# The clamp before the reciprocal norms: from VectorE's queue to GpSimd's

## The chip, the cores and the metric

One NeuronCore of one Trainium2 chip runs the whole program. The metric is the device time of one execution, in microseconds (us). In the profile the engines are called PE (TensorE's matmuls), PEld (its weight loads), DVE (VectorE), ACT (ScalarE), POOL (GpSimd) and SP (the queue that issues DMAs). L607 means line 607 of the kernel before.

## What is computed

The reference is a stack of four layers over x of 2 x 1024 tokens with 128 channels, each followed by a residual and a layer norm: attention, a mixture of experts, a state-space scan with a depthwise convolution, and a second mixture of experts with a shared expert. The change lies in the attention, which has 16 heads of 64 channels:

```python
def _l2norm(t):
    n = jnp.linalg.norm(t, axis=-1, keepdims=True)
    return t / jnp.maximum(n, 1e-12)

q = _l2norm(q) * jnp.exp(scale)
k = _l2norm(k)
sim = jnp.einsum('bhid,bhjd->bhij', q, k)
attn = jax.nn.softmax(sim, axis=-1)
out = jnp.einsum('bhij,bhjd->bhid', attn, v)
return out.transpose(0, 2, 1, 3).reshape(b, s, -1) @ w_out + b_out
```

The kernel computes 1 / max(n, 1e-12) as max(n squared, 1e-24) to the power -0.5. The maximum is the clamp that this case is about.

## The kernel before, in words

The function `attention` gives each engine one program of its own (one queue, carried out strictly in order) and ties them together by counting semaphores; the function `mixtures` does the other three layers behind it, in the same way. `Constants` holds small loads and tables that are made on the way.

The attention runs over pairs of heads (i from 0 to 7), each pair in 32 slots, that is 16 slots a head. A slot is one piece of the softmax: 256 queries against 512 keys. In each slot PE makes the scores into the PSUM bank pair SC (`scores`, L408 and L409), ACT takes the exponential into Pr (`exps`, L547), DVE takes the low half of the probabilities into Pl (`low_probs`, L644, one instruction of 128x1024), and three slots later PE multiplies Pr and Pl with the values into OP (`av`, L434 and L436, LAG = 3). SC has two buffers, Pr and Pl have PB = 5, and OP has two. After every second slot DVE reads OP (`read_out`: the reciprocal of the denominators L663 and the sum of the two parts L665), and POOL divides (`divide`, L756). The outputs are turned (L444), copied by ACT (L536), multiplied with w_out (`out_product`, L451) and added into x by DVE (`add_out`, L671); the next `out_product` and the next projection use the same bank M0 and wait for that addition.

Between these, all engines prepare the next head. PE projects q, k and v in eight pieces (`proj`, L375 to L377), ACT copies them to raw (L516) and squares them (L517), and the rest goes in four groups g. For each group DVE sums the squares (`square_sums`, L603) and clamps the sums (L607), POOL takes the power (`inverse_norms`, L764), DVE normalises (`normalize`, L617), rounds to 16 bits (`high_parts`, L626) and copies the keys (`copy_keys`, L631), POOL takes the low part (`low_parts`, L779), and PE turns the result (`transposes`, L390) for ACT to copy to QK (L529). POOL also takes the low part of the values (`low_values`, L772). In slots 20 and 28 of each pair DVE also makes a low part of weights for the later layers (`low_up`, L718), and ACT the high part in slots 18 and 26.

The slot in which a group is treated is written out by hand:

```python
SUM_AT = (1, 4, 6, 8)
NORM_AT = (4, 6, 8, 10)
VALUE_LOW_AT = (1, 4, 10, 15)
```

So the sums of group 1 are made in slot 4 and its normalisation in slot 6, group 2 in slots 6 and 8, group 3 in slots 8 and 10; group 0 has slots 1 and 4. The order inside a slot on DVE is: `low_probs`, `add_out` if there is one, `normalize`, `high_parts`, `copy_keys`, `square_sums`, and in even slots `read_out`, then `low_up`. On POOL it is: `low_values`, `low_parts`, `inverse_norms`, and in even slots `divide`. Between the sums of a group in slot 4 or 6 and its normalisation two slots later DVE thus does one `read_out` and two `low_probs`. Head 0 is prepared ahead of the slots, group after group; 15 heads are prepared inside them.

The tiles ss (sums), ss2 (clamped sums) and rn (reciprocal norms) have two buffers each, b = g % 2. The semaphores of this chain are s_squares, s_square_sums, s_clamped, s_inverse_norms and s_normalized, counted by G = 4h + g. The programs of the engines:

Of the kernel before, what the change touches and what calls it, by code (L numbers as in the profile page):

```python
# [8 lines left out]
ALU = mybir.AluOpType  # L9
# [21 lines left out]
def wait(eng, sem, count):  # L31

    if not isinstance(count, int) or count > 0:
        eng.wait_ge(sem, count)
# [49 lines left out]
def at_slot(place, s, n=PJ):  # L84

    return next((j for j in range(n) if place(j) == s), None)
# [113 lines left out]
def attention(nc, io, t):  # L200
# [3 lines left out]
    def sb(name, shape, dt):  # L204
        return es.enter_context(nc.sbuf_tensor(name, shape, dt))
# [4 lines left out]
    with es:  # L210
# [11 lines left out]
        ss = sb("ss", [P, 2, 4, 2], F32)  # L222
# [15 lines left out]
        ss2 = sb("ss2", [P, 2, 4, 2], F32)  # L238
# [28 lines left out]
        s_square_sums = sem("s_square_sums")  # L267
        s_clamped = sem("s_clamped")
        s_inverse_norms = sem("s_inverse_norms")
# [23 lines left out]
        def heads(eng, emit, constants=None):  # L293


            for s in range(2 * SLOTS):
                emit(0, s)
            for i in range(1, H // 2):
                for s in range(2 * SLOTS):
                    emit(i, s)  # L300
            for s in range(TAIL):
                emit(H // 2, s)
                if s == SLOTS // 2 and constants:
                    constants(eng)
# [13 lines left out]
        def ended(i):  # L318
            return isinstance(i, int) and i == H // 2

        def prepares(i, s):

            return not (isinstance(i, int) and 2 * i + s // SLOTS >= H - 1)

        def started(i, back):

            return not (isinstance(i, int) and i - back < 0)
# [4 lines left out]
        @block.sync  # L332
        def _(eng):
            for c in range(WCH):
                eng.dma_start(w_f32[:, chunk(c)], io["wqkv"][:, chunk(c)]).then_inc(s_w_loaded[c], 16)
                if c == 0:
                    for m in range(2):
                        cs = slice(S * m, S * m + S)
                        eng.dma_start(xT_f32[:, cs], io["xT"][:, cs]).then_inc(s_x_loaded[m], 16)
                    eng.dma_start(scl[:, :], io["scale"].partition_broadcast(P)).then_inc(s_loaded["scl"], 16)  # L340
            eng.dma_start(wo[:, :], io["wout"]).then_inc(s_loaded["wo"], 16)
            eng.dma_start(t["x"][:, :, :], io["x"].rearrange("(t p) d -> p t d", p=P)).then_inc(s_loaded["x"], 16)
            eng.dma_start(bout[:, :], io["b_out"].partition_broadcast(P)).then_inc(s_loaded["x"], 16)
            constants.sync(eng)

            def load(i):

                wait(eng, s_up_low, 2 * i)
                eng.dma_start(wst[:, :], io["up0"][:, bass.ds(2 * FF * i, 2 * FF)]).then_inc(s_up_loaded, 16)

            for i in range(H // 2):
                load(i)
# [246 lines left out]
        def _(eng):  # L599
            def square_sums(h, hb, g):  # L600
                G, b = 4 * h + g, g % 2
                wait(eng, s_squares, 8 * h + 2 * g + 2)
                eng.tensor_reduce(ss[:, b, :, :], sq[:, b, :, :, :], AX, ALU.add).then_inc(s_square_sums, 1)  # L603

                wait(eng, s_square_sums, G + 1)
                wait(eng, s_inverse_norms, G - 1)
                eng.tensor_scalar(ss2[:, b, :, :], ss[:, b, :, :], 1e-24, None, ALU.max).then_inc(s_clamped, 1)  # L607

            def normalize(h, hb, g):
                G, b = 4 * h + g, g % 2  # L610
# [71 lines left out]
            def prepare(h, hb, s):  # L682
                if s == 0:
                    head_scale(hb, h)
                if (g := at_slot(NORM_AT.__getitem__, s, 4)) is not None:
                    normalize(h, hb, g)
                    high_parts(h, hb, g)
                    copy_keys(h, hb, g)
                if (g := at_slot(SUM_AT.__getitem__, s, 4)) is not None:
                    square_sums(h, hb, g)  # L690
# [41 lines left out]
            eng.wait_ge(s_scales, 1)  # L732
            head_scale(0, 0)
            square_sums(0, 0, 0)
            for g in range(4):
                if g < 3:
                    square_sums(0, 0, g + 1)
                normalize(0, 0, g)
                high_parts(0, 0, g)
                copy_keys(0, 0, g)  # L740
                if g:
                    low_weights(g)
                    read_transposes(0, 0, 2 * (g - 1))
# [3 lines left out]
        @block.gpsimd  # L747
        def _(eng):
            def divide(i, s):

                b, u = s // SLOTS, s % SLOTS // 2
                m = 16 * i + 8 * b + u
                wait(eng, s_av_read, m + 1)
                wait(eng, s_inverse_sums, m + 1)

                eng.tensor_tensor(Ob[:, 2 * u:2 * u + 2, DH * b:DH * b + DH], osum[:, u % 2, :, :],  # L756
                                  rden[:, u % 4, :].unsqueeze(2).to_broadcast([P, 2, DH]), ALU.mult).then_inc(
                                      s_outputs, 1)

            def inverse_norms(h, hb, g):  # L760
                G, b = 4 * h + g, g % 2
                wait(eng, s_clamped, G + 1)
                wait(eng, s_normalized, G - 1)
                eng.tensor_tensor(rn[:, b, :, :], ss2[:, b, :, :],  # L764
                                  half[:, 0:1].unsqueeze(2).to_broadcast([P, 4, 2]), ALU.pow).then_inc(s_inverse_norms, 1)

            def low_values(h, hb, g):
                G, b = 4 * h + g, g % 2
                wait(eng, s_raw_read, 8 * h + 2 * g + 2)
                wait(eng, s_v_high, G + 1)  # L770
                v = V[:, hb, 4 * g:4 * g + 4, :]
                eng.tensor_tensor(v[:, :, DH + 1:2 * DH + 1], raw[:, g, :, 2 * DH:QKV], v[:, :, 0:DH],  # L772
                                  ALU.subtract).then_inc(s_v_low, 1)

            def low_parts(h, hb, g):
                G, b = 4 * h + g, g % 2
                wait(eng, s_qk_high, G + 1)
                both = stk[:, g, :, 0:4 * DH].rearrange("p t (k x) -> p t k x", k=2)
                eng.tensor_tensor(both[:, :, :, DH:2 * DH], nrm[:, b, :, :, :], both[:, :, :, 0:DH],  # L779
                                  ALU.subtract).then_inc(s_qk_low, 1)  # L780

            def prepare(h, hb, s):
                if (g := at_slot(VALUE_LOW_AT.__getitem__, s, 4)) is not None:
                    low_values(h, hb, g)
                if (g := at_slot(NORM_AT.__getitem__, s, 4)) is not None:
                    low_parts(h, hb, g)
                if (g := at_slot(SUM_AT.__getitem__, s, 4)) is not None:
                    inverse_norms(h, hb, g)

            def slot(i, s):  # L790
                h, sh = 2 * i + s // SLOTS, s % SLOTS
                if prepares(i, s):
                    prepare(h + 1, (s // SLOTS + 1) % 2, sh)
                if s % 2 == 0:
                    if s >= 4 and not ended(i):
                        divide(i, s - 4)
                    elif s < 4 and started(i, 1):
                        divide(i - 1, s + 2 * SLOTS - 4)

            for m in (t["ident16"], t["ident32"]):  # L800
                eng.memset(m[:, :], 0.0).then_inc(s_ident, 1)
            eng.memset(half[:, :], -0.5).then_inc(s_half, 1)
            eng.wait_ge(s_ident, 2)
            for m in (t["ident16"], t["ident32"]):
                eng.affine_select(out=m[:, :], in_=m[:, :], compare_op=ALU.not_equal, fill=1.0, base=0,
                                  pattern=[[-1, P]], channel_multiplier=1).then_inc(s_ident, 1)
            constants.clear(eng)
            eng.wait_ge(s_half, 1)
            inverse_norms(0, 0, 0)
            for g in range(4):  # L810
                if g < 3:
                    inverse_norms(0, 0, g + 1)
                low_values(0, 0, g)
                low_parts(0, 0, g)
            heads(eng, slot, constants.gpsimd)
# [930 lines left out]
```

## Time and profile before

| | us |
|---|---|
| median of 3 runs | 1154.01 (1152.89 to 1156.34) |
| the profiled execution's own time | 1161.62 |
| its span, first to last instruction | 1159.90 |
| PE busy | 940.8 (81%) |
| PEld busy | 863.8 (74%) |
| DVE busy | 770.5 (66%) |
| ACT busy | 775.9 (67%) |
| POOL busy | 538.7 (46%) |

The busy time of an engine is a sum over its instructions; a line of the profile names the engine, the source line, the operation, output and inputs, the shape and the count. What stands in square brackets behind an instruction is the idle time of its engine ahead of it and what ended it. Instructions of one engine overlap a little in the records: the next one's start can stand a few hundredths of a microsecond ahead of the end of the one before. The time of the profiled execution is 0.66% above the median, so sums are made against its own time and then carried over to the median.

The attention fills the span from its start to about 630 us; the heads' slots run from about 37 us on.

### The profile page before, as it was taken

The numbers are of one execution on the slowest core, as the hardware profiler recorded it, in microseconds if no ns is written. First come the engines' busy times: TensorE is split into PE (matmuls) and PEld (weight loads), VectorE is DVE, ScalarE is ACT, GpSimd is POOL, SyncE is SP. The second block draws the span as 40 slices with busy tenths as digits, with TensorE's granted clock in tenths as the row PEclk, the third lists the DMA queues.
The fourth block names the chain that finished last, engine by engine and source line by source line (L and its number), as shares of the span: only waits on it lengthen the run. The fifth ranks groups of instructions, "written<-read, shape, count | busy, mean of one in ns | idle before, by whom it ended". The sixth has DMA issues, their size and how long they took to land. (4 is left out here: it accounts for less than half of the span.)

```text
span 1159.9 us, 31023 instructions
## 1 busy us (share of the span) xinstructions
PE 940.8 (81%) x11628; PEld 863.8 (74%) x11628; DVE 770.5 (66%) x1495; ACT 775.9 (67%) x1279; POOL 538.7 (46%) x481
## 2 busy tenths in 40 slices
PE   3889999999999999999999419999765597977940
PEld 2788888889888888888888418888655497877840
DVE  6699988898889988998898514322379673320102
ACT  4789998889889888898886415333363455754841
POOL 5466665666557656566562164013270180032424
PEclk8899999999999999999999659999867688987975
DMA  8200000000000000000000331121110012012211
GB/s 274 73 2 20 2 2 20 3 20 2 2 20 3 2 20 2 20 2 2 20 3 3 163 98 45 43 68 47 29 34 1 3 35 60 25 42 76 65 51 43
DMA packets 42254, 41.89 MB, mean 36 GB/s; under 512 B 5505, under 2 KB 37249, under 8 KB 41729
## 3 DMA queue, kind: packets, MB, share of 16 engines
q1 hardware_dynamic: 38016, 31.51, 8.9%
q0 software_dynamic: 4096, 8.40, 2.5%
q8 instruction: 101, 1.65, 0.6%
q14 instruction: 41, 0.33, 0.1%
HBM read 25.60 MB, written 14.29 MB: 34 GB/s over the span
## 5 line engine op out<-in xcount | busy, mean ns | idle before, releaser
L644 DVE TENSOR_TENSOR Pl<-Pr 128x1024 f16<-128x1024 f32 x256 | 325.3, 1292 | 45.8 <-ACT Pr L547 44.5
L547 ACT ACTIVATE Pr<-SC,cur_nesc,cur_esc 128x1024 f32<-128x1024 f32 x256 | 308.5, 1208 | 28.7 <-issue 10.4
L408 PE MATMUL SC<-QK 128*128 128x256 f16 x1024 | 238.8, 274 | 1.0 <-ACT QK L529 1.0
L409 PE MATMUL SC<-QK 128*128 128x256 f16 x1024 | 238.9, 274 | 0.0
L434 PE MATMUL OP<-V,Pr 128*128 128x129 f16 x2048 | 212.0, 220 | 9.2 <-DVE osum L665 9.2
L436 PE MATMUL OP<-V,Pl 128*128 128x65 f16 x2048 | 205.3, 192 | 0.0
L434 PEld LDWEIGHTS OP<-V,Pr 128*128 128x128 bf16 x2048 | 183.9, 97 | 16.3 <-issue 13.5
L756 POOL TENSOR_TENSOR Ob<-osum,rden 128x128 f32<-128x128 f32 x128 | 133.2, 1041 | 109.8 <-DVE osum L665 109.1
L436 PEld LDWEIGHTS OP<-V,Pl 128*128 128x128 f16 x2048 | 180.9, 97 | 2.7
L1141 PE MATMUL DB<-wd,hid 128*128 (+1 forms) x864 | 133.0, 301 | 19.1 <-issue 6.1
L1141 PEld LDWEIGHTS DB<-wd,hid 128*128 128x128 f32 x864 | 113.8, 205 | 29.5 <-issue 27.9
L1630 POOL DMA_INDIRECT yg<-ys,slots x64 | 68.3, 1068 | 134.3 <-PE AB L1113 102.3
L529 ACT ACTIVATE QK<-M 128x768 f16<-128x768 f16 x124 | 100.3, 809 | 42.0 <-PE M L390 41.6
L1614 POOL DMA_INDIRECT xs<-split,slots x64 | 74.7, 1167 | 95.8 <-DVE slots L1435 52.4
L764 POOL TENSOR_TENSOR rn<-ss,half 128x8 f32<-128x8 f32 x64 | 107.5, 1679 | 16.5 <-DVE ss L607 11.5
L408 PEld LDWEIGHTS SC<-QK 128*128 128x128 f16 x1024 | 100.6, 98 | 10.3 <-issue 1.2
L409 PEld LDWEIGHTS SC<-QK 128*128 128x128 f16 x1024 | 100.6, 98 | 9.3
L779 POOL TENSOR_TENSOR stk<-nrm,stk 128x512 f16<-128x512 f32 x64 | 75.1, 1173 | 62.3 <-DVE stk L626 62.3
L1460 DVE TENSOR_TENSOR hid<-act,UB 128x512 f32<-128x512 f32 x46 | 31.7, 688 | 104.4 <-PE UB L1123 99.3
L772 POOL TENSOR_TENSOR V<-raw,V 128x256 f16<-128x256 f32 x64 | 64.5, 1007 | 66.1 <-ACT V L524 66.1
L1528 DVE TENSOR_TENSOR_SCAN st<-scratch 128x1024 f32<-128x1024 f32 x32 | 71.8, 2278 | 24.2 <-ACT scratch L1285 20.4
L390 PE MATMUL M<-ident,stk 128*128 128x128 f16 x768 | 65.9, 224 | 20.5 <-issue 9.0
(195 smaller groups left out, 2103.5 us busy)
## 6 DMA issues: line engine op xcount, KB each, us to landing
ys<-yb SPq DMA_DIRECT2D x92, 64.0 KB
xg<-xs SPq DMA_DIRECT2D x12, 384.0 KB, 4.4
wst<-in_up SPq DMA_DIRECT2D x8, 512.0 KB
xs<-zero SPq DMA_DIRECT2D x2, 1472.0 KB
scratch<-in_up SPq DMA_DIRECT2D x1, 2304.0 KB, 8.7
wd<-in_wd SPq DMA_DIRECT2D x1, 2304.0 KB, 13.7
wd<-in_wd SPq DMA_DIRECT2D x1, 2048.0 KB
QK<-in_wqkv SPq DMA_DIRECT2D x4, 384.0 KB, 7.2
```

The costliest lines, as they stand in the source:

```text
L408: eng.matmul(out, QK[:, b, 1, key:key + P], rhs, start=True, stop=False)
L409: mm = eng.matmul(out, QK[:, b, 2, key:key + P], rhs, start=False, stop=True)
L434: eng.matmul(OP[u % 2][:, at:at + 129], hi, V[:, b, tile, 0:129], start=first, stop=False, skip_group_check=True)
L436: mm = eng.matmul(OP[u % 2][:, at:at + 65], lo, V[:, b, tile, 0:65], start=False, stop=last, skip_group_check=True)
L529: eng.activation(QK[:, hb, :, 2 * P * j:2 * P * j + 2 * P], M1[:, :].bitcast(F16)[:, 0:6 * P].rearrange("p (k c) -> p k c", k=3), ACT.Copy ...
L547: eng.activation(Pr[:, n % PB, :, :], SC[s % 2][:, :, :], ACT.Exp, bias=cur_nesc[:, b:b + 1], scale=cur_esc[:, b:b + 1]).then_inc(s_exps, 1)
L644: eng.tensor_tensor(Pl[:, n % PB, :, :].rearrange("p a b -> p (a b)"), pr, high(pr)[:, 1::2], ALU.subtract).then_inc(s_low_probs, 1)
L756: eng.tensor_tensor(Ob[:, 2 * u:2 * u + 2, DH * b:DH * b + DH], osum[:, u % 2, :, :], rden[:, u % 4, :].unsqueeze(2).to_broadcast([P, 2, D ...
L764: eng.tensor_tensor(rn[:, b, :, :], ss2[:, b, :, :], half[:, 0:1].unsqueeze(2).to_broadcast([P, 4, 2]), ALU.pow).then_inc(s_inverse_norms, 1)
L779: eng.tensor_tensor(both[:, :, :, DH:2 * DH], nrm[:, b, :, :, :], both[:, :, :, 0:DH], ALU.subtract).then_inc(s_qk_low, 1)
L1141: mm = eng.matmul(DB[:, 0:D], hid[:, u % HR, P * c:P * c + P], wd[l][:, bass.ds(first + P * c, P)], start=c == 0, stop=c == NC - 1)
L1614: eng.indirect_dma_start(out=xs[b], out_offset=bass.IndirectOffsetOnAxis(ap=slots[:, b, k, i:i + 1], axis=0), in_=split[:, b, i, :], in_of ...
```

## The change

The instruction that clamps the sums moves from the end of DVE's `square_sums` to the head of POOL's `inverse_norms`, with its two waits. The instruction itself is the same (128 partitions x 8 values, f32 to f32). DVE's sum gets a wait of its own for the clamp of the group two before, since the buffer of ss is no longer read by DVE's own queue. The power still waits for s_clamped, which POOL now raises itself.

```diff
             def square_sums(h, hb, g):
                 G, b = 4 * h + g, g % 2
                 wait(eng, s_squares, 8 * h + 2 * g + 2)
+                wait(eng, s_clamped, G - 1)
                 eng.tensor_reduce(ss[:, b, :, :], sq[:, b, :, :, :], AX, ALU.add).then_inc(s_square_sums, 1)
-
-                wait(eng, s_square_sums, G + 1)
-                wait(eng, s_inverse_norms, G - 1)
-                eng.tensor_scalar(ss2[:, b, :, :], ss[:, b, :, :], 1e-24, None, ALU.max).then_inc(s_clamped, 1)
...
             def inverse_norms(h, hb, g):
                 G, b = 4 * h + g, g % 2
+                wait(eng, s_square_sums, G + 1)
+                wait(eng, s_inverse_norms, G - 1)
+                eng.tensor_scalar(ss2[:, b, :, :], ss[:, b, :, :], 1e-24, None, ALU.max).then_inc(s_clamped, 1)
                 wait(eng, s_clamped, G + 1)
                 wait(eng, s_normalized, G - 1)
                 eng.tensor_tensor(rn[:, b, :, :], ss2[:, b, :, :],
```

## Rows read from the trace of the kernel before

**Rows 1.** 58 to 600 us: busy PE, PEld, DVE, ACT, POOL, then PE's granted clock

```profile
58.00:600.00 542.00, 504.56 (x7184) 470.50 (x7181) 500.45 (x841) 475.15 (x697) 338.87 (x288) 1.00 0.03 9
```

**Rows 2.** Waits, 58 to 600 us: who waited for whom, total, times, longest

```profile
PE M L451 <- issue: 11.9, 19, 1.0
...
PE OP L434 <- DVE osum L665: 9.2, 17, 1.1
...
PE M L375 <- DVE x L671: 7.5, 6, 1.3
```

**Rows 3.** Timeline of PE: start, us, instruction, idle before

```profile
214.00 0.22 PE L434 MATMUL OP<-V,Pr 128*128 128x129 f16 x1 [0.31 <-DVE osum L665]
...
217.34 0.68 PE L451 MATMUL M<-wo,OT 128*128 128x128 f32 x4 [0.58 <-issue]
```

**Rows 4.** Timeline of DVE, slots 4 to 10 of a pair (its even head's)

```profile
195.43 0.68 DVE L617 TENSOR_TENSOR nrm<-raw,rn 128x512 f32<-128x512 f32 x1
...
197.03 0.67 DVE L603 TENSOR_REDUCE ss<-sq 128x8 f32<-128x512 f32 x1
...
200.76 0.89 DVE L617 TENSOR_TENSOR nrm<-raw,rn 128x512 f32<-128x512 f32 x1
...
202.22 0.68 DVE L603 TENSOR_REDUCE ss<-sq 128x8 f32<-128x512 f32 x1
202.94 0.44 DVE L607 TENSOR_SCALAR ss<-ss 128x8 f32<-128x8 f32 x1
...
203.69 2.34 DVE L644 TENSOR_TENSOR Pl<-Pr 128x1024 f16<-128x1024 f32 x2
205.96 0.88 DVE L617 TENSOR_TENSOR nrm<-raw,rn 128x512 f32<-128x512 f32 x1
...
211.64 1.14 DVE L617 TENSOR_TENSOR nrm<-raw,rn 128x512 f32<-128x512 f32 x1
```

**Rows 5.** Timeline of POOL in the same stretch

```profile
202.19 1.16 POOL L779 TENSOR_TENSOR stk<-nrm,stk 128x512 f16<-128x512 f32 x1 [1.09 <-DVE stk L626]
203.45 1.63 POOL L764 TENSOR_TENSOR rn<-ss,half 128x8 f32<-128x8 f32 x1
```

**Rows 6.** All powers: duration in ns, smallest, median, largest

```profile
L764 POOL TENSOR_TENSOR rn<-ss,half x64: 1627/1634/2663, 13.0 to 589.7; 128x8 f32<-128x8 f32 x64
```

**Rows 7.** Timelines of DVE and POOL where the power started second

```profile
43.16 2.36 DVE L644 TENSOR_TENSOR Pl<-Pr 128x1024 f16<-128x1024 f32 x2
...
43.22 2.66 POOL L764 TENSOR_TENSOR rn<-ss,half 128x8 f32<-128x8 f32 x1 [0.36 <-DVE ss L607]
...
78.74 1.21 DVE L644 TENSOR_TENSOR Pl<-Pr 128x1024 f16<-128x1024 f32 x1
...
78.90 2.54 POOL L764 TENSOR_TENSOR rn<-ss,half 128x8 f32<-128x8 f32 x1
```

**Rows 8.** Timelines of DVE and POOL around the end of L779, slots 10 and 11

```profile
213.77 3.14 DVE L644 TENSOR_TENSOR Pl<-Pr 128x1024 f16<-128x1024 f32 x2
...
213.33 1.16 POOL L779 TENSOR_TENSOR stk<-nrm,stk 128x512 f16<-128x512 f32 x1 [1.08 <-DVE stk L626]
214.44 1.39 POOL L756 TENSOR_TENSOR Ob<-osum,rden 128x128 f32<-128x128 f32 x1
```

**Rows 9.** POOL's one instruction of the clamp's kind and size

```profile
L175 POOL TENSOR_SCALAR starts<-iota x1: 250/250/250, 633.7 to 633.7; 128x8 f32<-128x8 f32 x1
```

**Rows 10.** Timeline of DVE, slots 20 to 26 (the odd head's)

```profile
232.91 0.69 DVE L617 TENSOR_TENSOR nrm<-raw,rn 128x512 f32<-128x512 f32 x1
...
235.97 0.68 DVE L718 TENSOR_TENSOR w0l<-wst,w0h 128x512 f16<-128x512 f32 x1
...
239.05 0.68 DVE L617 TENSOR_TENSOR nrm<-raw,rn 128x512 f32<-128x512 f32 x1
...
244.09 0.89 DVE L617 TENSOR_TENSOR nrm<-raw,rn 128x512 f32<-128x512 f32 x1
...
249.61 1.17 DVE L617 TENSOR_TENSOR nrm<-raw,rn 128x512 f32<-128x512 f32 x1
```

## The prediction, made before the changed kernel ran

> **What bounds the kernel now.** I read the busy times first. Over the heads' slots PE is busy 504.6 of 542 us (93%), DVE 500.5 (92%), ACT 475.2 (88%) and POOL 338.9 (63%), at a granted clock of 1.00 [rows 1]. So three engines run nearly full and only POOL looks free, which makes a move from DVE to POOL look cheap. The waits come next: PE's matmuls wait 9.2 us in all for DVE's read of the outputs, 7.5 us for an addition into x by DVE, and 11.9 us ahead of the output product with no releaser named [rows 2]. Of that last kind the timeline shows one that ends 0.1 us after an addition L671 on DVE (out_product waits for add_out), so I count it as a wait for DVE too [rows 3]. PE is thus the engine that sets the pace, and late in each head it is held back by DVE.
>
> The third reading is DVE itself. From the normalisation in slot 4 to the one in slot 10 (195.43 to 211.64) the rows follow each other without a bracket, so DVE has no idle time there; a delay that it gets in this stretch it still has when PE comes to wait for it at 214.00 and 217.34 [rows 3, 4]. The odd head looks the same from 232.91 to 249.61 [rows 10]. Whatever delays a normalisation in slots 6 to 10 therefore goes into the time, and so would whatever advances it, up to PE's waits.
>
> **What the change takes off DVE.** 64 clamps; in the dense stretch one is 0.44 us and shifts what follows by some 0.47 us: the sum ends at 202.90, the clamp starts at 202.94, and the low part that started at 203.69 would start at 203.22 [rows 4]. Three clamps a head lie in the dense stretch; that of group 0 lies where DVE waits for ACT anyway, and taking it away gives nothing. Its move costs nothing either: the power of group 0 (slot 1) has until slot 4, over 4 us, which covers a delay of 1 or 2 us.
>
> **What it adds to POOL.** The only row of this kind and size on POOL is 0.25 us [rows 9]; above it, the power of the same shape, 1.63 us, is the far bound [rows 6], and below it nothing. I take 0.25, since it is the same kind of instruction. The new wait of DVE's sum is for a clamp two groups back, some 5 us old, and costs nothing. POOL's busy share would rise by 64 x 0.25 = 16 us, which its idle time holds.
>
> **Where the price lies: the place of the power.** A power takes 1.63 us in the median [rows 6]. The two rows where it started inside a low-part instruction of DVE are longer: at 43.22 it took 2.66 us beside a pair of L644 that began at 43.16 and whose first half ended at 44.34 (43.16 + 2.36/2), so it ended 1.54 us after that end; at 78.90 it took 2.54 us, and ended 1.49 us after the L644 that had started at 78.74 [rows 7]. So a power that comes second waits for the end of the L644 and then takes 1.5 us. They are the longest of all (the largest is this 2663 ns [rows 6]), and where the others started no such instruction of DVE was under way but in four cases outside the slots or at their start, which obey the same. A head start of 0.06 us was enough (43.16 against 43.22). Where the power comes first, L644 runs beneath it at its usual 1.17 us (203.45 against 203.69) [rows 4, 5]. Before the change the power wins this race by 0.24 us.
>
> After the change it can't. The clamp goes ahead of it, and L644 comes 0.47 us earlier. With R the end of the sum (202.90), L644 is issued at R + 0.32, while POOL is in L779 until 203.35, R + 0.45. POOL's next instruction starts 0.05 us ahead of that end (214.44 against 213.33 + 1.16) [rows 8], so the clamp is issued at R + 0.41 at the earliest, behind L644. Rows 8 show what comes of this order: L644, issued during L779, took 3.14 us a pair in place of 2.34, and POOL's next instruction, of 128x128, took 1.39, more than the 1.16 of L779 with four times the elements; POOL got in only between the two L644. So: first L644 from R + 0.45 to R + 1.62; the clamp between it and the second; the power is issued after the clamp's end, some 0.1 us behind the second L644, and waits for that one's end, R + 1.62 + 1.17 + 0.1 = R + 2.9; it ends at R + 4.4, and the normalisation starts at R + 4.45. A clamp of up to 1.1 us would hide in this.
>
> On the waits of an instruction that comes second the Trainium skill, "SBUF — State Buffer", section "Who interferes with whom", says that a VectorE instruction with two SBUF inputs contends with a GpSimd instruction that reads SBUF, and that the one that issues first holds the shared ports for its whole instruction. On the waiting side the trace agrees (1.5 us after the L644's end, twice); on the holding side it doesn't, since by that rule a power of 1.63 us would have blocked the L644 pair at 203.69, which took 2.34 us, its usual time.
>
> Now the six windows of a pair, from one normalisation to the next. R is 2.14 us after the start of a normalisation (200.76 to 202.90), 2.27 in the first window of a head (195.43 to 197.70) [rows 4].
> - slots 4 to 6: 2.27 + 4.45 = 6.72 for 5.33 now (200.76 - 195.43), +1.39.
> - slots 6 to 8: 2.14 + 4.45 = 6.59 for 5.20, +1.39.
> - slots 8 to 10: here an addition (L671) of 0.33 us stands between the two L644 and takes nothing from POOL, so the power may get in. If it does, 2.14 + 1.62 + 0.35 + 1.55 = 5.7 for 5.68, nothing; if not, 6.8, +1.1. I take half, +0.55 [rows 4].
> - slots 20 to 22: L718 of 0.68 us goes first, the clamp follows it, and the power waits for one L644 only: 2.27 + 0.45 + 0.68 + 1.17 + 1.55 = 6.12 for 6.14, nothing; +1.17 if it waits for both [rows 10].
> - slots 22 to 24: 6.59 for 5.04, +1.55; slots 24 to 26: 6.59 for 5.52, +1.07 [rows 10].
>
> That is 5.95 us a pair. POOL's division stands right behind the power and reads ahead of the normalisation; five times some 0.1 us, +0.5. So 6.4 us a pair, and 7.5 pairs are prepared in slots: 48 us. Head 0 ahead of them has four more POOL instructions in a chain that POOL nearly fills: 4 x 0.25 = +1 us (0 to 3). **Sum: +49 us**, all of it path, since DVE has no idle time in these stretches and PE already waits behind them. Against the profiled execution's own 1161.62 that is 1210.6; carried over to the median of 1154.01, 7.6 below it, 1203 us, 4.2% slower.
>
> **The rivals.**
> *The clamp gets in first.* The order at L779's end hangs on 0.1 us. If POOL's clamp reads ahead of the first L644, the power waits for one L644 only: it ends at R + 0.45 + 0.1 + 1.17 + 1.5 = R + 3.2, and the normalisation starts at R + 3.27, against R + 3.06 now (205.96 - 202.90). The windows change by +0.2, +0.2, -0.3, -0.4, +0.4 and -0.1; with the divisions that is within 0.5 us of nothing a pair: 1150 to 1158, 1154. For it speaks the thin margin, against it that 0.06 us decided rows 7.
> *A clean gain.* Clamp and power both read before the first L644, or an instruction of 8 values a partition isn't held up. Then DVE is 0.47 us earlier three times in each of 15 heads, 21 us; that is also the sum of PE's waits for it (9.2 + 11.9 [rows 2]), so at most 1154 - 20 = 1134. Against it: the power has the same 8 values and is held up in rows 7.
> *The whole instruction holds.* By the skill's rule, taken in full and with the clamp first, the power that follows the first L644 would keep the second one waiting for its 1.5 us, and the time would come out near the forecast. Worked from rows: first L644 to R + 1.72, power to R + 3.3, second L644 to R + 4.5, so again +1.4 us a window and about 1200. The 2.34 us of rows 4 speak against it.
>
> **How the numbers follow.** My forecast has 0.66. Its own range: without the halves taken in slots 8 to 10 and without the divisions, 5.4 x 7.5 = +40; with 1.1 in slots 8 to 10, 1.17 in slots 20 to 22 and the 3 us of head 0, 8.1 x 7.5 + 3 = +64: 1194 to 1218. The clamp first has 0.20, the clean gain 0.11, the whole-instruction case 0.03. A change of 0.3%, 3.5 us, is about what a measurement of this kernel can tell. Clamp-first splits into 0.12 same, 0.05 faster and 0.03 slower. So faster 0.16, same 0.12, slower 0.72. The range takes in the forecast's own and clamp-first's, 1150 to 1218, and leaves out the clean gain and the tails.
>
> **What would show it.** In the profile of the changed kernel the power should take about 2.6 to 2.8 us in slots 4, 6 and in 22, 24 in place of 1.63, the clamp on POOL over 1 us in place of 0.25 (it waits for the first L644), and DVE should wait 1 to 1.5 us for the power ahead of L617, a wait that the trace of before doesn't have; PE's waits for DVE should grow by some 3 us a head. It is wrong if the powers stay at 1.63, or if they are long and L617 is still not late, which would mean that PE's and ACT's waits had covered it.

## The result, and the profile after

The changed kernel takes 1189.19 us in the median of 6 runs (1186.69 to 1194.12), the kernel before 1152.50 in 6 runs beside it: a ratio of 1.0317 (95% interval 1.0292 to 1.0341), or 36.7 us slower. The profiled execution took 1188.93 us. Of all the runs below one, of e4_power_first, took 5127 us; it is left out of that kernel's median and ratio.

The page of the changed kernel, busy times over the whole span (the counterpart of the table ahead), and the same stretch of the slots as in [rows 1]:

```profile
span 1187.1 us, 31085 instructions
...
PE 938.5 (79%) x11628; PEld 857.4 (72%) x11628; DVE 751.6 (63%) x1431; ACT 778.6 (66%) x1279; POOL 599.2 (50%) x545
...
58.00:600.00 542.00, 477.46 (x6757) 440.68 (x6756) 456.00 (x740) 449.58 (x654) 373.88 (x326) 1.00 0.03 9
```

DVE lost the 64 clamps and 19 us of busy time; POOL gained 64 and 60 us, nearly four times the 16 of 64 x 0.25. In the same 542 us PE does less, 477 us for 505 in [rows 1], at the same granted clock.

The waits between 58 and 600 us (who waited for whom, total, times, longest) say where it went:

```profile
DVE nrm L614 <- POOL rn L764: 47.1, 41, 1.6
...
PE OP L434 <- DVE osum L662: 37.6, 36, 2.4
...
PE M L451 <- issue: 12.8, 18, 1.0
...
PE M L375 <- DVE x L668: 7.6, 6, 1.3
```

The first line is new: the normalisation waits for the power, up to 1.6 us. The second is the wait of [rows 2] that was 9.2 us; it is 28 us longer, while the other two of [rows 2] hardly moved. Now all clamps and all powers, durations in ns (smallest, median, largest), to be held against [rows 6] and [rows 9]:

```profile
L761 POOL TENSOR_SCALAR ss<-ss x64: 238/1222/1232, 12.7 to 625.9; 128x8 f32<-128x8 f32 x64
...
L764 POOL TENSOR_TENSOR rn<-ss,half x64: 1664/2473/2642, 13.1 to 627.2; 128x8 f32<-128x8 f32 x64
```

Nearly all are of two kinds, free (0.24 and 1.67) and held up (1.22 and 2.47); in slots 20, behind L718, the clamp takes 0.69. The timelines of DVE and POOL over slots 6 to 10 show why; they answer to [rows 4, 5]:

```profile
214.01 0.88 DVE L614 TENSOR_TENSOR nrm<-raw,rn 128x512 f32<-128x512 f32 x1 [1.56 <-POOL rn L764]
...
215.47 0.68 DVE L604 TENSOR_REDUCE ss<-sq 128x8 f32<-128x512 f32 x1
...
216.47 2.35 DVE L641 TENSOR_TENSOR Pl<-Pr 128x1024 f16<-128x1024 f32 x2
220.37 0.88 DVE L614 TENSOR_TENSOR nrm<-raw,rn 128x512 f32<-128x512 f32 x1 [1.55 <-POOL rn L764]
...
222.83 1.22 DVE L641 TENSOR_TENSOR Pl<-Pr 128x1024 f16<-128x1024 f32 x1
223.96 0.41 DVE L668 TENSOR_TENSOR x<-x,M 128x256 f32<-128x256 f32 x1
224.29 1.22 DVE L641 TENSOR_TENSOR Pl<-Pr 128x1024 f16<-128x1024 f32 x1
225.93 0.88 DVE L614 TENSOR_TENSOR nrm<-raw,rn 128x512 f32<-128x512 f32 x1 [0.42 <-POOL rn L764]
```

```profile
215.44 1.16 POOL L779 TENSOR_TENSOR stk<-nrm,stk 128x512 f16<-128x512 f32 x1 [1.09 <-DVE stk L623]
216.56 1.23 POOL L761 TENSOR_SCALAR ss<-ss 128x8 f32<-128x8 f32 x1
217.87 2.47 POOL L764 TENSOR_TENSOR rn<-ss,half 128x8 f32<-128x8 f32 x1
220.31 0.40 POOL L753 TENSOR_TENSOR Ob<-osum,rden 128x128 f32<-128x128 f32 x1
221.80 1.16 POOL L779 TENSOR_TENSOR stk<-nrm,stk 128x512 f16<-128x512 f32 x1 [1.09 <-DVE stk L623]
222.92 1.23 POOL L761 TENSOR_SCALAR ss<-ss 128x8 f32<-128x8 f32 x1
224.23 1.67 POOL L764 TENSOR_TENSOR rn<-ss,half 128x8 f32<-128x8 f32 x1
```

With R = 216.15, the end of the sum L604: L641 (the former L644) is issued at R + 0.32, the clamp at R + 0.41. The clamp ends at 217.79, just behind the end of the first of the pair (216.47 + 2.35/2 = 217.65). The power, issued at 217.87, ends at 220.34, 1.52 us behind the pair's end at 218.82. The normalisation starts at 220.37, R + 4.22. In slot 8 the first L641 is alone, the addition L668 follows, and the power, issued 0.06 us ahead of the second L641, takes 1.67: DVE waits 0.42 us only.

Behind the attention nothing is changed. The copies of the head scales, one for each head, with their first and last start (L678 before, then L675 after):

```profile
L678 DVE COPY cur_esc<-esc x16: 141/147/149, 10.1 to 567.9; 128x1 f32<-128x1 f32 x16
```

```profile
L675 DVE COPY cur_esc<-esc x16: 141/147/148, 10.0 to 601.9; 128x1 f32<-128x1 f32 x16
```

The last head's comes 34.0 us later, so the loss lies ahead of it. The two profiled executions differ by less in all, 27.3 us: that of the kernel before was 7.6 us above its median and this one is at its own. The difference lies behind the heads: from that last copy to the end of the span the kernel before took 592.0 us and the changed one 585.2, with the same program there; over all the traces this rest lies between 580.9 and 595.2.

### The profile page after: what moved, and what is told of

It reads as the page before. It is cut to its first block and busy times, and to the rows that moved or that the text cites. A ratio compares the mean times of both kernels' runs of the same rounds, so it can differ in the third digit from the quotient of the medians.

```text
span 1187.1 us, 31085 instructions
## 1 busy us (share of the span) xinstructions
PE 938.5 (79%) x11628; PEld 857.4 (72%) x11628; DVE 751.6 (63%) x1431; ACT 778.6 (66%) x1279; POOL 599.2 (50%) x545
## 5 line engine op out<-in xcount | busy, mean ns | idle before, releaser
L641 DVE TENSOR_TENSOR Pl<-Pr 128x1024 f16<-128x1024 f32 x256 | 323.0, 1284 | 48.7 <-ACT Pr L547 47.2
L753 POOL TENSOR_TENSOR Ob<-osum,rden 128x128 f32<-128x128 f32 x128 | 106.0, 828 | 105.1 <-DVE osum L662 103.8
L764 POOL TENSOR_TENSOR rn<-ss,half 128x8 f32<-128x8 f32 x64 | 139.8, 2184 | 5.3
L1141 PE MATMUL DB<-wd,hid 128*128 (+1 forms) x864 | 130.1, 296 | 11.2 <-DVE x L1466 3.5
L1141 PEld LDWEIGHTS DB<-wd,hid 128*128 128x128 f32 x864 | 111.2, 201 | 21.4 <-issue 19.5
L779 POOL TENSOR_TENSOR stk<-nrm,stk 128x512 f16<-128x512 f32 x64 | 75.5, 1180 | 44.1 <-DVE stk L623 44.1
L614 DVE TENSOR_TENSOR nrm<-raw,rn 128x512 f32<-128x512 f32 x64 | 54.5, 851 | 54.3 <-POOL rn L764 54.3
```

The costliest lines, as they stand in the source:

```text
L641: eng.tensor_tensor(Pl[:, n % PB, :, :].rearrange("p a b -> p (a b)"), pr, high(pr)[:, 1::2], ALU.subtract).then_inc(s_low_probs, 1)
L764: eng.tensor_tensor(rn[:, b, :, :], ss2[:, b, :, :], half[:, 0:1].unsqueeze(2).to_broadcast([P, 4, 2]), ALU.pow).then_inc(s_inverse_norms, 1)
L1141: mm = eng.matmul(DB[:, 0:D], hid[:, u % HR, P * c:P * c + P], wd[l][:, bass.ds(first + P * c, P)], start=c == 0, stop=c == NC - 1)
```

## The experiments

All were timed beside the kernel before on the same chip; its median there stands with each group, and the ratio is what to compare. Two theories went in. A: the clamp makes the power lose its place ahead of DVE's L644, and it then waits for that instruction's end. B: the clamp costs what it takes, and what its hand-over takes, on POOL, 36.7 us over 64 clamps. The expectations were worked out from the 1152.5 us of the kernel before; on another chip their ratios are held against the measured ones. The `tensor_scalar` named in the diffs is the clamp.

**No clamp** (e1_no_clamp), on the changed kernel; the sum's wait for s_clamped also becomes one for s_inverse_norms, with the same count:

```diff
-                wait(eng, s_inverse_norms, G - 1)
-                eng.tensor_scalar(ss2[:, b, :, :], ss[:, b, :, :], 1e-24, None, ALU.max).then_inc(s_clamped, 1)
-                wait(eng, s_clamped, G + 1)
                 wait(eng, s_normalized, G - 1)
-                eng.tensor_tensor(rn[:, b, :, :], ss2[:, b, :, :],
+                eng.tensor_tensor(rn[:, b, :, :], ss[:, b, :, :],
```

> The clamp is left out: POOL's power reads the sums themselves. Theory A (place in the race): the price of the change is that the power comes behind an L644 of DVE. Without the clamp it comes behind the first one only and ends at R + 1.62 + 1.5 = R + 3.1, near the R + 3.06 at which the normalisation starts in the kernel before. Powers of about 2.6 us in the even slots, almost no wait of DVE for the power, 1146 us (1140 to 1153). Theory B (the clamp's own time and hand-over on POOL is the price): without it the power follows L779 at once and takes 1.63, DVE is 0.47 us earlier three times a head, 1132 us (1128 to 1138).

Measured: 1152.54 us beside 1160.66, ratio 0.9926 (0.9901 to 0.9952), 8 us faster than before and not the 20 of theory B. All powers, and one with its DVE row:

```profile
L761 POOL TENSOR_TENSOR rn<-ss,half x64: 1627/2618/2627, 12.6 to 581.5; 128x8 f32<-128x8 f32 x64
```

```profile
201.05 2.36 DVE L641 TENSOR_TENSOR Pl<-Pr 128x1024 f16<-128x1024 f32 x2
...
201.14 2.62 POOL L761 TENSOR_TENSOR rn<-ss,half 128x8 f32<-128x8 f32 x1
```

With no clamp anywhere the power still takes 2.62 us in the median, since DVE without its clamp issues L641 0.09 us ahead of it. It waits for one L641 in place of two, and DVE waits 0.39 us for the power. So the 0.47 us that DVE saves in a window is lost again to the same race where two L641 follow each other: in slots 6 to 8 the window is 5.19 us for 5.20 before. The gain of this kernel comes from other windows, in this pair 5.20 for 5.68 in slots 8 to 10 and 5.48 for 6.14 in slots 20 to 22.

**A wait more** (e2_wait_clamp), on the changed kernel, in the slots and for groups 1 to 3:

```diff
                 eng.tensor_reduce(ss[:, b, :, :], sq[:, b, :, :, :], AX, ALU.add).then_inc(s_square_sums, 1)
+                if inside and g:
+                    wait(eng, s_clamped, G + 1)
```

> The changed kernel with one more wait: behind the sums of groups 1 to 3, DVE waits for the clamp on POOL before it reads OP, so that clamp and power are both issued ahead of the next L644. Theory A: clamp 0.25 us, power 1.63 us again, DVE waits some 0.7 us for the clamp where it saved 0.47 us, so about +0.3 us a window and 6 windows a pair against the kernel before: 1165 us (1156 to 1172), some 24 us faster than the changed kernel although a wait was added. Theory B: the chain on POOL is as long as before and DVE has a wait more, 1189 us or more.

Measured: 1177.63 us beside 1160.66, ratio 1.0164 (1.0119 to 1.0208): about 17 us above the kernel before where the changed kernel is 36.7 above. Theory A's ratio was 1.011 (1.003 to 1.017), so this is at its upper end. Timelines of DVE and POOL, slots 6 to 8:

```profile
208.59 0.68 DVE L604 TENSOR_REDUCE ss<-sq 128x8 f32<-128x512 f32 x1
209.96 0.17 DVE L662 RECIPROCAL rden<-OP 128x2 f32<-128x2 f32 x1 [0.69 <-POOL ss L763]
...
210.37 2.35 DVE L643 TENSOR_TENSOR Pl<-Pr 128x1024 f16<-128x1024 f32 x2
212.63 0.89 DVE L616 TENSOR_TENSOR nrm<-raw,rn 128x512 f32<-128x512 f32 x1
...
209.68 0.24 POOL L763 TENSOR_SCALAR ss<-ss 128x8 f32<-128x8 f32 x1
210.01 1.67 POOL L766 TENSOR_TENSOR rn<-ss,half 128x8 f32<-128x8 f32 x1
```

Clamp 0.24 and power 1.67 us: both are issued ahead of the pair, which runs beneath the power at its usual 2.35, and the normalisation follows without idle time. An added wait of 0.69 us took away one of 1.55. Theory B gives no reason for this.

**The clamp of one group on POOL**, the others on DVE, with a semaphore of its own (on the kernel before; shown for group 0):

```diff
+        ON_POOL = (0,)
...
+                if g in ON_POOL:
+                    return
                 wait(eng, s_square_sums, G + 1)
...
+                if g in ON_POOL:
+                    wait(eng, s_square_sums, G + 1)
+                    wait(eng, s_inverse_norms, G - 1)
+                    eng.tensor_scalar(ss2[:, b, :, :], ss[:, b, :, :], 1e-24, None, ALU.max).then_inc(
+                        s_clamped_pool, 1)
```

> The kernel before, with the clamp of group 0 alone (slot 1 of each head, and one ahead of the slots) on POOL. Theory A: the power of group 0 has over 4 us until it is needed and DVE isn't dense there: as before, 1152.5 us (1149 to 1156). Theory B, a price for each clamp on POOL (36.7 us over 64): a quarter of it, 1162 us.

Measured for group 0 (slot 1): 1160.18 us beside 1160.66, ratio 0.9996 (0.9982 to 1.0010). Nothing, as its cover said.

> The kernel before, with the clamp of group 2 alone on POOL (slot 6 of each head). Theory A (the power loses its place ahead of the L644 pair): only the windows from slot 6 to 8 and 22 to 24 grow, by what they grew in the changed kernel, 1.16 and 1.33 us: 2.5 us a pair, 7.5 pairs, +19 us (14 to 23) on the kernel before; clamps and powers of that group 1.2 and 2.5 us, the others unchanged. An equal price for each of the 64 clamps would give a quarter of the change's, +9.

Measured for group 2 (slot 6): 1172.27 us beside 1152.81, ratio 1.0168 (1.0152 to 1.0183), +19.5 us for 16 instructions. POOL's rows over slots 4 to 8:

```profile
205.20 1.63 POOL L781 TENSOR_TENSOR rn<-ss,half 128x8 f32<-128x8 f32 x1
210.26 1.22 POOL L775 TENSOR_SCALAR ss<-ss 128x8 f32<-128x8 f32 x1
211.56 2.47 POOL L781 TENSOR_TENSOR rn<-ss,half 128x8 f32<-128x8 f32 x1
216.75 1.63 POOL L781 TENSOR_TENSOR rn<-ss,half 128x8 f32<-128x8 f32 x1
```

Only the power behind POOL's own clamp is long.

> The kernel before, with the clamp of group 3 alone on POOL (slot 8). Theory A: in the even heads an addition without a second SBUF input stands between the two L644 and the power gets in there, in the odd ones it doesn't; the windows change by -0.13 and +0.84 us as in the changed kernel: 0.7 us a pair, +5 us (2 to 9). An equal price for each clamp: +9.

Measured for group 3 (slot 8): 1161.39 us beside 1152.81, ratio 1.0075 (1.0061 to 1.0088), +8.6 us, at the upper end of the 2 to 9 of theory A. In the first head that is prepared in slots no addition stands between the two L644, and its window grows by 1.2 us (6.37 for 5.18), which the expectation left out. The run doesn't by itself part A from B, which expected 9. The three runs together do: 0, 19.5 and 8.6 for equal numbers of the same instruction. Group 1 wasn't run alone; if the groups add up, 36.7 less these leaves it 8.6.

**The power first, without the clamp** (e4_power_first), on e1_no_clamp; s_qk_low is raised by POOL's L779, the instruction ahead of the power:

```diff
+                if prepares(i, s) and sh in NORM_AT[:3]:
+
+                    wait(eng, s_qk_low, 4 * (h + 1) + NORM_AT.index(sh) + 1)
                 if s in UP_LOW_AT and not ended(i):
```

> As e1_no_clamp (the clamp is left out), and in slots 4, 6 and 8 DVE waits, behind its read of OP, for the low part L779 on POOL of the same slot. POOL's power is then issued some 0.1 us ahead of L644. Theory A: the power takes 1.63 us, L644 starts some 0.1 us later than without the wait, since L779 held it up anyway, and DVE keeps 0.4 us of the 0.47 three times in each of 15 heads: 1136 us (1131 to 1143), faster than e1_no_clamp by about 10. Theory B: an added wait gives nothing, the same as e1_no_clamp or slower.

Measured: 1146.50 us beside 1160.66, ratio 0.9877 (0.9841 to 0.9912), 6.0 us faster than without the wait on the same chip. About 10 were expected; the ratio is inside the one of theory A, 0.986 (0.981 to 0.992). Timelines of DVE and POOL, slot 6:

```profile
197.70 0.68 DVE L604 TENSOR_REDUCE ss<-sq 128x8 f32<-128x512 f32 x1
...
198.86 2.36 DVE L641 TENSOR_TENSOR Pl<-Pr 128x1024 f16<-128x1024 f32 x2
201.14 0.89 DVE L614 TENSOR_TENSOR nrm<-raw,rn 128x512 f32<-128x512 f32 x1
...
197.66 1.17 POOL L779 TENSOR_TENSOR stk<-nrm,stk 128x512 f16<-128x512 f32 x1 [1.09 <-DVE stk L623]
198.78 1.64 POOL L764 TENSOR_TENSOR rn<-ss,half 128x8 f32<-128x8 f32 x1
```

The power leads by 0.08 us and is 1.64 us long. The wait costs DVE 0.16 us (L641 at R + 0.48 in place of R + 0.32).

**The clamp in a third place** (e5_min_in_norm and e6_min_power_first): the reciprocal norm is limited inside the normalisation, which computes all of the reference, since the smaller of 1/n and 1e12 is 1 / max(n, 1e-12). As in e1_no_clamp POOL's clamp is taken out and the sum's wait is changed. e6_min_power_first has the wait of e4_power_first as well.

```diff
-                eng.tensor_tensor(nrm[:, b, :, :, :], qk, rn[:, b, :, :].unsqueeze(3).to_broadcast([P, 4, 2, DH]),
-                                  ALU.mult).then_inc(s_normalized, 1)
+                eng.scalar_tensor_tensor(out=nrm[:, b, :, :, :],
+                                         in0=rn[:, b, :, :].unsqueeze(3).to_broadcast([P, 4, 2, DH]), scalar=1e12,
+                                         in1=qk, op0=ALU.min, op1=ALU.mult).then_inc(s_normalized, 1)
```

> The clamp is made in another place: the reciprocal norm is limited to 1e12 inside the normalisation (minimum and product in one instruction of DVE), and the power reads the sums. This computes all of the reference. Theory A: as e1_no_clamp if the two-step instruction takes what the product took, 0.69 to 0.88 us: ratio to before 0.993 (0.989 to 0.998), powers of 2.6 us.

> e5_min_in_norm, with the wait of e4_power_first ahead of L644 in slots 4, 6 and 8. All of the reference is computed. Theory A: as e4_power_first, powers of 1.63 us, DVE 0.3 us earlier a window: ratio to before 0.988 (0.984 to 0.993), faster than both the kernel before and the changed one. A wait that only costs would give more than e5_min_in_norm.

Measured: 1144.66 us and 1138.24 us beside 1152.81, ratios 0.9929 (0.9915 to 0.9943) and 0.9871 (0.9856 to 0.9887). The second beats the kernel before by 14.6 us and the changed one by more. Groups of the second: the two-step instruction costs what the product cost (0.86 us in the mean, in e4_power_first and here), and the powers are short.

```profile
L765 POOL TENSOR_TENSOR rn<-ss,half 128x8 f32<-128x8 f32 x64 | 106.5, 1664 | 10.7 <-DVE ss L604 10.7
...
L614 DVE SCALAR_TENSOR_TENSOR nrm<-rn,raw 128x512 f32<-128x512 f32 x64 | 55.0, 860 | 0.3 <-POOL rn L765 0.3
```

**A wait for the wrong instruction** (e9_wait_before_low), on the changed kernel:

```diff
+                if prepares(i, s) and sh in SUM_AT[1:]:
+
+                    wait(eng, s_clamped, 4 * (h + 1) + SUM_AT.index(sh) + 1)
                 if s in UP_LOW_AT and not ended(i):
```

> The changed kernel with a wait of DVE for the clamp, as in e2_wait_clamp, but placed behind the read of OP, right ahead of the next L644 or L718 in slots 4, 6 and 8. The clamp then goes first (0.25 us), and its end, some R + 0.66, releases the power on POOL (0.08 us later by the trace of the changed kernel) and L644 on DVE (0.07 us later by the kernel before) nearly at once. Theory A: if L644 wins, the power takes 1.2 + 1.5 = 2.7 us and the windows grow by some 0.4 us: ratio to before 1.01 to 1.02; if the power wins it takes 1.63 and the time is that of the kernel before, ratio 0.998 to 1.004. Theory B (the chain on POOL is as long in any case): 1.03 or more.

Measured: 1173.62 us beside 1159.14, ratio 1.0122 (1.0096 to 1.0148), the case in which L644 wins. Timelines of DVE and POOL, slots 4 to 6:

```profile
203.07 2.36 DVE L641 TENSOR_TENSOR Pl<-Pr 128x1024 f16<-128x1024 f32 x2 [0.29 <-POOL ss L764]
205.85 0.88 DVE L614 TENSOR_TENSOR nrm<-raw,rn 128x512 f32<-128x512 f32 x1 [0.42 <-POOL rn L767]
...
202.79 0.24 POOL L764 TENSOR_SCALAR ss<-ss 128x8 f32<-128x8 f32 x1
203.12 2.70 POOL L767 TENSOR_TENSOR rn<-ss,half 128x8 f32<-128x8 f32 x1
```

The clamp is free now (0.24 us), and the power, 0.05 us behind L641, takes 2.70. Against the changed kernel this is the same clamp and the same power with one L641 to wait for in place of two. The wait stands at the same place as in e4_power_first; it differs in what it is for. The clamp ends at 203.03, and both L641 and the power have waited for it: L641 starts 0.04 us behind that end, the power 0.09. In e4_power_first the power has nothing to wait for when L779 ends (198.83); it starts 0.05 us ahead of that end and L641 0.03 behind it.

## Why the prediction was right, and where a size was off

It forecast slower, 1203 us, with a range of 1150 to 1218; 1189.19 was measured. That is 5 us below the 1194 to 1218 that the forecast's own mechanism was given, and it lies in the stated range only because that took in the times of a rival that didn't happen: in this the prediction was lucky. The mechanism was right and its size too large, 49 us (40 to 64) where the runs beside each other show 36.7; the other 1.5 us come from the kernel before, 1152.50 in these runs for the 1154.01 that the sum was put on. Of its signs, the clamp (1.22 us) and DVE's wait for the power (1.55) came as said; the powers take 2.47 for 2.6 to 2.8, and PE's wait for DVE grew by some 2 us a head for 3. By its steps:

- **DVE in the dense stretch has no cover.** Right: what the six windows of a pair grew is found again in PE's wait for L662, 37.6 us for 9.2. The windows of the changed kernel are 6.50, 6.36, 5.56, 5.96, 6.37 and 6.36 us, 37.11 in all for 32.91 before [rows 4, 10], +4.20; a pair of heads takes 80.56 us for 76.19, +4.37, and 7.5 x 4.37 = 33 us.
- **Who comes first.** Right to 0.01 us: L641 at R + 0.32, the clamp at R + 0.41. The rival in which the clamp gets in first, and the clean gain, had no instance in slots 4, 6, 22 and 24 of any pair. e1_no_clamp, e2_wait_clamp and e9_wait_before_low turned the order around and back, and the power followed each time.
- **Two L644 in the way, power 2.6 to 2.8 us.** The waiting is right; the size is the term that was too large. I had the first L644 start at R + 0.45, at the end of L779. It isn't held: the pair that was issued at R + 0.32 took 2.35 us, its usual time, and ended at R + 2.67, not R + 2.9. So the normalisation starts at R + 4.22, not 4.45: 0.23 us too much in each of four windows.
- **Slots 8 to 10.** I took half of 0 to +1.1. The power gets in behind the addition, and the window is 5.56 for 5.68. Slots 20 to 22 came as forecast, 5.96 for 6.14, since L718 goes first and the power waits for one L644 less; 0.18 less is counted as 0.2 below.
- **The divisions**, +0.5 a pair, aren't there: the normalisation behind the division takes 0.88 us as before. With these the 6.45 us a pair of the sum become 6.45 - 0.9 - 0.7 - 0.2 - 0.5 = 4.2, which is what the windows grew.
- **Head 0**: +1 us was too little. The first exponential comes 2.3 us later (39.59 for 37.29), since clamps and powers are held up there too: the third clamp, at 19.14, takes 0.56 us and its power 2.26, for 1.81 before.
- **The move of group 0 is free.** Right, and run alone: 0.9996.
- **The holding side of the Trainium skill's rule.** By the Trainium skill, "SBUF — State Buffer", section "SBUF: two separate sides", whichever of a VectorE instruction with two SBUF inputs and a GpSimd one that reads SBUF starts first holds the shared ports for its whole instruction; the prediction had named another section of that page and had set the rule against [rows 4, 5]. In e2_wait_clamp a power of 1.67 us had been issued 0.36 us ahead of a pair of L643 that took 2.35 us, the same as without one. The measurement decides: a power of 8 values a partition, issued first, doesn't visibly hold up the VectorE instruction behind it. On the waiting side the trace agrees: behind L641 the power ended 1.5 us after the end of the VectorE instruction in this kernel (1.52), in e1_no_clamp (1.53) and in e9_wait_before_low (1.57).

That two instructions compete for ports is the Trainium skill's reading, not shown here; the runs show that the power's length depends on whether it is issued ahead of or behind L644, by 0.05 to 0.09 us. e3_pool_group0 shows no price of the moved instruction and its waits where they have cover. No run replaced L644 by an instruction with one input in SBUF; the nearest row is that of slot 8, where the power issued during the addition L668, whose second input M lies in PSUM, took 1.67.

## What to carry to other kernels

Before a small instruction is moved to a less busy engine, look at what runs on the other engine at the moment in which it will start, and at who is first by how much: here 64 instructions of 0.25 us, 16 us of work for which POOL had idle time enough, cost 37 us, because two instructions of POOL came behind DVE's long ones where one had come just ahead. Where the order is lost by a few hundredths of a microsecond, a wait that lets the small one go first can be worth more than it costs (6 us in e4_power_first, some 20 in e2_wait_clamp against the changed kernel), but only if the small one really is issued first. Either the wait stands ahead of a short piece of work of the waiting engine (e2_wait_clamp), or it is for the instruction just ahead of the small one, which then follows with nothing to wait for (e4_power_first). Where both engines were released by the same instruction, the small one lost by 0.05 us (e9_wait_before_low). The cheapest clamp was in neither of the two places: it was folded into an instruction that was there anyway.

## What the runs showed of the hardware that wasn't expected

Removing an instruction from the busy engine made the other engine's next one longer: with no clamp the power went from 1.63 to 2.62 us in the median. The low part of DVE that was issued 0.13 us ahead of the end of POOL's L779 wasn't held up at all (2.35 us a pair), while one issued 0.72 us ahead of it was [rows 8]; so in these two rows L779 no longer holds DVE up at 0.13 us ahead of its recorded end. And an instruction of 8 values a partition is held up like a large one when it comes second: the clamp took 1.22 us for 0.24. When it comes first it doesn't hold DVE up, as L779 does: the power of e2_wait_clamp left the pair its 2.35 us, and L779 made one of 3.14 [rows 8].
